# The residual of the first stage enters the down products on TensorE, and GpSimd builds it

## What is computed

```python
# weights are 4-bit codes: _dequant(codes, scales) = table[code] * scale of its block of 64
q, k, v = (_lin_lora(x, W[i], A[i], B[i]) for i in range(3))
attn = (q + k + v) / 3.0
o = _lin_lora(attn, W_o, A_o, B_o)
x1 = x + o
g = _lin_lora(x1, W_g, A_g, B_g)        # 512 -> 1792
u = _lin_lora(x1, W_u, A_u, B_u)
h = silu(g) * u
d = _lin_lora(h, W_d, A_d, B_d)         # 1792 -> 512
x = _layernorm(x + x1 + d)              # stage 1; then a 4-bit linear, an attention, a mixture of experts
```

## Time and profile before

| | |
|---|---|
| Median of 3 runs | 532.95 us (532.86 to 535.76) |
| Profiled execution, span from first to last instruction | 532.1 us |
| PE busy | 494.5 us, 93% |
| DVE busy | 379.4 us, 71% |
| ACT busy | 293.9 us, 55% |
| POOL busy | 251.6 us, 47% |
| Mean granted TensorE clock | 0.993 of full speed |

### The profile page before, as it was taken

One profiled execution on the slowest core, in us unless ns is written; L12 is line 12 of the kernel. 1 busy time (PEld: TensorE's weight loads), 2 busy tenths in 40 slices (PEclk: granted clock), 3 DMA queues, 4 the chain that ended last, 5 costly groups with the idle time before them and its releaser, 6 DMA issues.

```text
span 532.1 us, 7568 instructions
## 1 busy us (share of the span) xinstructions
PE 494.5 (93%) x2278; PEld 394.7 (74%) x2278; DVE 379.4 (71%) x716; ACT 293.9 (55%) x541; POOL 251.6 (47%) x252
## 2 busy tenths in 40 slices
PE   2968999788999999999999999899998899999995
PEld 0236678567888888888888888688886788888874
DVE  4888898666789789797987983577457966366442
ACT  6688856676666576666674742158487422332021
POOL 3357702465566576665674753147479410110001
PEclk9999999899999999999999999999999999999998
DMA  6575421243233333343333300740000000000011
GB/s 169 173 263 159 139 59 41 79 139 100 80 106 75 96 105 118 82 119 97 105 115 97 103 19 0 267 155 5 1 1 1 2 2 19 21 20 22 0 41 39
DMA packets 21415, 43.01 MB, mean 81 GB/s; under 512 B 3328, under 2 KB 3456, under 8 KB 21120
## 3 DMA queue, kind: packets, MB, share of 16 engines
q1 hardware_dynamic: 21152, 42.15, 25.6%
q0 software_dynamic: 224, 0.38, 0.3%
HBM read 40.42 MB, written 2.10 MB: 80 GB/s over the span
## 4 chain that ended last, share of the span: by engine, by line
PE 69%; ACT 3%; issue 3%; DVE 2%; POOL 0%; POOLq 0%; ACTq 0%; DVEq 0%
PE bank L996 62%; PE bank L1162 3%; PE bank L1009 2%; PE bank L1266 1%; ACT prob L957 1%; ACT pT_hi L780 1%; PE bank L1018 0%; DVE rmax L1480 0%; DVE pT_lo L1306 0%; ACT eb_hi L780 0%; ACT bank L785 0%; DVE rows L1413 0%; POOL gu_lo L740 0%; ACT v_hi L780 0%; PE bank L1025 0%
## 5 line engine op out<-in xcount | busy, mean ns | idle before, releaser
L718 POOL TENSOR_TENSOR wf<-value,scale 128x512 f32<-128x512 f32 x50 | 64.5, 1290 | 93.1 <-DVE value L1338 93.1
L996 PE MATMUL bank<-x_hi,gu_hi 128*128 128x512 f32 x224 | 89.9, 401 | 1.7 <-POOL gu_lo L740 1.7
L996 PE MATMUL bank<-x_lo,gu_hi 128*128 128x512 f32 x224 | 88.2, 394 | 0.0
L996 PE MATMUL bank<-x_hi,gu_lo 128*128 128x512 f32 x224 | 88.1, 393 | 0.0
L763 POOL TENSOR_TENSOR rstd<-veps,neg_half 128x1 f32<-128x1 f32 x32 | 17.6, 549 | 121.8 <-issue 110.5
L785 ACT ACTIVATE bank<-code 128x512 f32<-128x512 int32 x124 | 68.7, 587 | 0.0
L1316 DVE SCALAR_TENSOR_TENSOR low<-bent,bank 128x512 f32<-128x512 f32 x62 | 42.5, 685 | 24.0 <-ACT bank L785 19.4
L746 POOL TENSOR_TENSOR h_lo<-act_f,h_hi 128x512 fp32r<-128x512 f32 x28 | 36.3, 1297 | 31.7 <-ACT h_hi L780 31.7
L1413 DVE SCALAR_TENSOR_TENSOR rows<-bank,rows 128x512 f32<-128x512 f32 x48 | 33.0, 688 | 24.7 <-PE bank L996 24.3
L996 PEld LDWEIGHTS bank<-x_hi,gu_hi 128*128 128x128 f32 x224 | 42.6, 190 | 9.9 <-issue 2.1
L996 PEld LDWEIGHTS bank<-x_hi,gu_lo 128*128 128x128 f32 x224 | 42.5, 190 | 9.1
(11 more groups left out here) (198 smaller groups left out, 1172.7 us busy)
## 6 DMA issues: line engine op xcount, KB each, us to landing
code<-codes SPq DMA_DIRECT2D x62, 256.0 KB, 2.7
scale<-scales SPq DMA_DIRECT2D x100, 128.0 KB, 3.0
xs<-xT SPq DMA_DIRECT2D x2, 1024.0 KB, 5.6
ea_raw<-ex_A SPq DMA_DIRECT2D x1, 2048.0 KB, 9.9
eb_raw<-ex_B SPq DMA_DIRECT2D x1, 2048.0 KB, 7.5
out<-rows SPq DMA_DIRECT2D x8, 256.0 KB, 2.0
bgu_raw<-loB_gu SPq DMA_DIRECT2D x1, 896.0 KB, 4.7
wqkv_raw<-w_qkv SPq DMA_DIRECT2D x1, 768.0 KB, 4.3
```

The source lines that it names most:

```text
L718: pool.tensor_tensor(w, v, scale[:, i % RING_CODES, :], ALU.mult).then_inc(scaled_done, 1)
L996: last = nc.tensor.matmul(ps, a, b, start=start and i == 0 and n == 0, stop=stop and i == len(terms) - 1 and n == 2)
```

## The change

Three edits belong together. (1) The item "res" is gone. `down(0, t)` first issues the four transpositions of `xs` for its 128 tokens into its bank, as the start of the accumulation, and the six matmuls add to them. ScalarE then copies the bank to `rows`, where VectorE had added it. (2) The transposed residual can't be divided by GAIN in the bank, so the down weights no longer carry it: their merge divides by GAIN, and the adds of the later rounds lose the factor. (3) VectorE's add of x1 to `xs` is gone. In its place stands an item "xs" in V, at the places that the items "res" had, on which GpSimd adds first `x1_hi` and then `x1_lo` to `xs`; the second add waits for the first. TensorE's waits for `xs_done` ahead of the second batch and of the first products become waits for `x1lo_done` or go; `down(0, t)` waits for `xs_done`. Diff, with unchanged context cut:

```diff
@@ -199,22 +199,22 @@
     half(("u", 1), 0)
     half(("u", 1), 1)
     half(("d", 0), 0)
-    order += [("silu", 0), ("res", 0)]
+    order += [("silu", 0), ("xs", 0)]
     half(("d", 0), 1)
     unit_h(0)
-    order.append(("res", 1))
+    order.append(("xs", 1))
     half(("d", 1), 0)
-    order += [("silu", 1), ("res", 2)]
+    order += [("silu", 1), ("xs", 2)]
     half(("d", 1), 1)
     unit_h(1)
-    order.append(("res", 3))
+    order.append(("xs", 3))
     for f in range(1, NF):
         downs = downs_beside(f) + [None] * 4
         ahead = [(m, f + 1) for m in "gud"] if f < NF - 1 else []
         ahead += [("f", FFN_AT[f])] if f in FFN_AT else []
         halves = [(c, part) for c in ahead for part in range(2)]
         if f == 1:
-            downs = [("res", t) for t in range(TPB, TT)]
+            downs = [("xs", n) for n in range(KT, NB * KT)]
         steps = (("silu", 2 * f), downs[0], ("h", 2 * f), downs[1], ("silu", 2 * f + 1), downs[2],
                  ("h", 2 * f + 1), downs[3])
         if f == 4:
@@ -243,16 +243,11 @@
     return ([None] if f == 2 else []) + downs[max(start, 0):max(start + 4, 0)]
 
 
-def res_beside(f):
-
-    return [("res", 4 * f + i) for i in range(4)] if f < 2 else []
-
-
 def tensor_order():
     order = []
     held = ("d", 1)
     for f in range(NF):
-        downs = (res_beside(f) or downs_beside(f)) + [None] * 4
+        downs = downs_beside(f) + [None] * 4
         ahead = [(m, f + 1) for m in "gud"] if 1 <= f < NF - 1 else []
         late = ("f", FFN_AT[f]) if f in FFN_AT else None
         if f == 0:
@@ -732,6 +726,18 @@
                     pool.wait_ge(xhi_done, item[1] + 1)
                     pool.tensor_tensor(x_lo[:, k, tk], xs[:, k, tk], x_hi[:, k, tk].bitcast(F32), ALU.subtract)\
                         .then_inc(xlo_done, 1)
+                elif kind == "xs":
+                    n = item[1]
+                    b, o = n // KT, n % KT
+                    tk = slice(b * SEQ, (b + 1) * SEQ)
+                    pool.wait_ge(xhi_done, KT * (b + 1))
+                    pool.wait_ge(x1hi_done, n + 1)
+                    pool.tensor_tensor(xs[:, o, tk], xs[:, o, tk], x1_hi[:, o, tk].bitcast(F32), ALU.add)\
+                        .then_inc(xs_step, 1)
+                    pool.wait_ge(x1lo_done, n + 1)
+                    pool.wait_ge(xs_step, n + 1)
+                    pool.tensor_tensor(xs[:, o, tk], xs[:, o, tk], x1_lo[:, o, tk].bitcast(F32), ALU.add)\
+                        .then_inc(xs_done, 1)
                 elif kind == "split":
                     c = item[1]
                     hi, lo = dest(c)
@@ -870,11 +876,11 @@
                     act.wait_ge(x1_ready, NB * KT)
                     copy(la_fhi[:, :], la_f[:, :], fprep_hi)
                     copy(lb_fh[:, :], lb_f[:, :], fprep_hi)
-                elif kind == "res":
-                    t = item[1]
-                    act.wait_ge(res_ready, t + 1)
+                elif kind == "down" and not item[1]:
+                    t = item[2]
+                    act.wait_ge(down_ready, t + 1)
                     act.wait_ge(bprep_done, 2)
-                    copy(rows[:, t, :], bank[7][:, :], res_set)
+                    copy(rows[:, t, :], down_bank(0, t)[:, :], down_added)
                 elif kind == "silu":
                     n = item[1]
                     act.wait_ge(gate_ready, n + 1)
@@ -1085,7 +1091,7 @@
             for n in range(KT, NB * KT):
                 r = n - KT
                 pe.wait_ge(x1hi_done, n - 3)
-                pe.wait_ge(xs_done, n - 3)
+                pe.wait_ge(x1lo_done, n - 3)
                 cut = slice(r * P, (r + 1) * P)
                 product(mm_ps[r][:, :], [(m1_hi[:, k, cut], m1_lo[:, k, cut], x_hi[:, k, SEQ:], x_lo[:, k, SEQ:])
                                          for k in range(KT)]).then_inc(x1_ready, 1)
@@ -1101,7 +1107,6 @@
                     seen = (KT + 1, KT + 2, NB * KT)[m]
                     pe.wait_ge(x1hi_done, seen)
                     pe.wait_ge(x1lo_done, seen)
-                    pe.wait_ge(xs_done, seen)
                 elif m > 2 and g == 0:
                     pe.wait_ge(h_done, n - 1)
                 elif m > 2:
@@ -1116,8 +1121,6 @@
 
                 n = gi * TT + t
                 last_f = GROUPS[gi][-1]
-                if n == 0:
-                    pe.wait_ge(res_set, TT)
                 if gi == len(GROUPS) - 1 and t == 1:
                     pe.wait_ge(h_done, 2 * NF)
                 elif gi == len(GROUPS) - 1 and t > 1:
@@ -1130,29 +1133,20 @@
                 pe.wait_ge(lo_done, split_no(("d", last_f)))
                 tk = slice(t * P, (t + 1) * P)
                 ps = down_bank(gi, t)
+                if gi == 0:
+                    pe.wait_ge(xs_done, KT * (t // TPB + 1))
+                    for k in range(KT):
+                        nc.tensor.matmul(ps[:, k * P:(k + 1) * P], xs[:, k, tk], ident[:, :], is_transpose=True,
+                                         start=k == 0, stop=False)
                 product(ps[:, :], [(h_hi[:, f % RING_H, tk], h_lo[:, f % RING_H, tk],
                                     wd_hi[:, f % RING_H, :], wd_lo[:, f % RING_H, :])
-                                   for f in GROUPS[gi]]).then_inc(down_ready, 1)
-
-            def res(t):
-
-                pe.wait_ge(xs_done, NB * KT)
-                pe.wait_ge(x1hi_done, NB * KT)
-                pe.wait_ge(x1lo_done, NB * KT)
-                if t:
-                    pe.wait_ge(res_set, t)
-                tk = slice(t * P, (t + 1) * P)
-                for k in range(KT):
-                    last = nc.tensor.transpose(bank[7][:, k * P:(k + 1) * P], xs[:, k, tk], ident[:, :])
-                last.then_inc(res_ready, 1)
+                                   for f in GROUPS[gi]], start=gi > 0).then_inc(down_ready, 1)
 
             for item in filter(None, T):
                 if item[0] == "lora":
                     lora(item[1])
                 elif item[0] == "down":
                     down(item[1], item[2])
-                elif item[0] == "res":
-                    res(item[1])
                 else:
                     unit(item[1], item[0] == "up")
 
@@ -1349,7 +1343,10 @@
                     w = wf[:, j % RING_W, :]
                     weight_wait(dve, c)
                     dve.wait_ge(lora_ready, i + 1)
-                    if c[0] != "f":
+                    if c[0] == "d":
+                        nc.vector.scalar_tensor_tensor(w, w, 1.0 / GAIN, lora_ps[:, :], ALU.mult, ALU.add)\
+                            .then_inc(lora_added, 1)
+                    elif c[0] != "f":
                         nc.vector.scalar_tensor_tensor(w, lora_ps[:, :], GAIN, w, ALU.mult, ALU.add)\
                             .then_inc(lora_added, 1)
                     else:
@@ -1374,8 +1371,6 @@
                     dve.wait_ge(x1hi_done, n + 1)
                     dve.wait_ge(xlo_done, KT * (b + 1))
                     rest(x1_lo[:, o, tk], mm_ps[n % 4][:, :], x1_hi[:, o, tk], x1lo_done)
-                    nc.vector.tensor_tensor(xs[:, o, tk], mm_ps[n % 4][:, :], xs[:, o, tk], ALU.add)\
-                        .then_inc(xs_done, 1)
                 elif kind == "bprep":
 
                     i = item[1]
@@ -1402,16 +1397,13 @@
                     dve.wait_ge(unit_ready, n + 1)
                     nc.vector.scalar_tensor_tensor(a, unit_ps[(2 * n + 1) % 3][:, :], 1.0 / GAIN, a, ALU.mult, ALU.mult)\
                         .then_inc(h_done, 1)
-                elif kind == "down":
+                elif kind == "down" and item[1]:
                     gi, t = item[1:]
                     n = gi * TT + t
                     dve.wait_ge(down_ready, n + 1)
-                    if gi == 0:
-                        dve.wait_ge(res_set, t + 1)
-                    else:
-                        dve.wait_ge(down_added, (gi - 1) * TT + t + 1)
-                    nc.vector.scalar_tensor_tensor(rows[:, t, :], down_bank(gi, t)[:, :], 1.0 / GAIN, rows[:, t, :],
-                                                   ALU.mult, ALU.add).then_inc(down_added, 1)
+                    dve.wait_ge(down_added, (gi - 1) * TT + t + 1)
+                    nc.vector.tensor_tensor(rows[:, t, :], down_bank(gi, t)[:, :], rows[:, t, :], ALU.add)\
+                        .then_inc(down_added, 1)
 
             for item in TAIL:
                 kind = item[0]
@@ -1420,8 +1412,7 @@
                     n = gi * TT + t
                     dve.wait_ge(down_ready, n + 1)
                     dve.wait_ge(down_added, (gi - 1) * TT + t + 1)
-                    nc.vector.scalar_tensor_tensor(rows[:, t, :], down_bank(gi, t)[:, :], 1.0 / GAIN, rows[:, t, :],
-                                                   ALU.mult, ALU.add)\
+                    nc.vector.tensor_tensor(rows[:, t, :], down_bank(gi, t)[:, :], rows[:, t, :], ALU.add)\
                         .then_inc(down_added, 1)
                 elif kind == "stat":
```

(3 more changed lines are left out.)

## The result

| | before | changed | ratio, 95% interval |
|---|---|---|---|
| first comparison, median | 533.91 us (4 runs) | 551.73 us (548.83 to 551.85, 4 runs) | 1.0306 [1.0274, 1.0339] |
| second comparison, median | 534.70 us (27 runs) | 548.12 us (546.68 to 549.72, 4 runs) | 1.0246 [1.0209, 1.0282] |
| span of the first profiled execution | 532.1 us | 546.9 us | |

The page of the changed kernel, part 1, answers to the earlier trace rows: TensorE is busy 5.2 us longer in a span that is 14.8 us longer, VectorE has 10.8 us less to do and GpSimd 19.2 us more.

The account below looks back on a forecast made before the run. GpSimd's program order was taken to delay TensorE, which then runs without gaps: 7.96 queue + 2.13 clock + 3.6 transpositions + 1.0 ScalarE = 14.7 us on a 532.1 us span, 546.8, written as time 547.5 us, range 540 to 552.

Parts of the forecast that it names:

- GpSimd's queue: GpSimd from 94.2 us: 16 instructions plus eight add pairs take 41.0 us; f = 2's first up product starts 7.96 us later.
- Clock: TensorE's pauses before f = 2's first up product lower its clock for about 4.26 us behind them: 2.13 us lost.
- Transpositions: Eight groups of four now stand in TensorE's first down round, without gaps, at 0.45 us each: 3.6 us.
- ScalarE's new place: ScalarE's copies wait for TensorE's down groups, delaying later up weights: about 1.0 us of TensorE stall.
- The sum: Whole span: 7.96 + 2.13 + 3.6 + 1.0 = 14.7 us on 532.1, giving 546.8 us.
- From span to time: Whole kernel: the median of the runs stands 0.85 us above the span, so 546.8 becomes 547.6, written 547.5.
- the case that the queue binds: GpSimd's instruction order sets the start of f = 2's first up product as worked out: 542 to 551 us, chance 0.78.
- not slower: Rival: adds hide in GpSimd's idle time; 532 us, or 524 to 528 with all earlier TensorE pauses gone; chance 0.09.
- the GpSimd queue fills less: Rival: GpSimd's adds take 1.04 us each; about 543 us, or 541 without clock loss; chance 0.08.
- Stretched adds: Rival: GpSimd's adds meet VectorE's two-SBUF-input instructions and take 7.4 us more in all, 555 us; chance 0.05.

Follow-up runs that it names:

- the run with one add: Changed kernel with one GpSimd add for each xs item instead of two, the low part of x1 left out: 538.16 us, ratio 1.0076 to before.
- the filler run: Changed kernel with idle matmuls into unused bank 7 in TensorE's three pauses, GpSimd's queue untouched: 549.05 us, ratio 1.0293 to before.
- the items apart: Changed kernel with the xs items moved in the order, none beside the LoRA factor preparation on VectorE, two late: 539.38 us, ratio 1.0078 to before.
- the run with the items spread: Changed kernel with the same sixteen adds moved to places where GpSimd had been idle: 537.28 us, ratio 1.0055 to before.
- the run with dprep later: Changed kernel, x1 added by VectorE, fprep earlier, plus LoRA down-factor preparation moved behind the merge of g 1: 535.42 us, ratio 1.0017 to before.

## Why the prediction was right, and where it was off

The forecast was slower, 547.5 us, between 540 and 552; measured were 551.73 and 548.12. By its steps, in the first profile:

- **GpSimd's queue.** Predicted 41.0 us from 94.2, up 4 at 135.35, 7.96 us late; measured 41.23 us from 94.21, up 4 at 135.59, 8.20 us late. The pair took 2.68 us against 2.62: the adds are 1.285 us as the row of the same operation said, but between the two there are 0.15 us (98.19 - 96.76 - 1.28) where the nearest row had 0.08. Against VectorE's 0.682 us the ratio is 1.9, so the row gave the sum. The Trainium skill, GPSIMD Engine Reference, section 4.1 (Engine selection), calls GpSimd about 2x slower for two inputs; the trace agrees nearly, with 1.9. That the queue and not the rest of the change sets up 4 was argued then; the run with x1 on VectorE and the run with one add show it.
- **Clock.** Predicted 2.13 us, measured 4.44 - 2.85 = 1.6. The sign and the mechanism hold (the filler run); the size was misread. I took half of the 4.26 us, as if all of it ran at the lower level, but the mean clock of that row is 0.62, which loses 0.38 x 4.26 = 1.6 us. The pauses were not where I had put them: about 5.5, 3 and 4 us, and in the trace 5.55 before the lora step ahead of up 3, 0.83 before gate 4, and 5.79 before up 4. I had not reckoned that up 3 itself runs slow and fills the gap before gate 4. That the row of 1.9 us without loss gives no bound for pauses under 3 us is shown by the runs with one add (2.98 us) and with the items apart (2.24 us), which both lost clock, and a longer pause gives no certainty either (the last section).
- **Transpositions.** Predicted 3.6 us. From up 4 to up 8 the trace has 41.45 us against 35.06 before: 6.39 more, of which 1.6 are clock and 0.82 the wait of up 8, so 3.97. Leaving them out gave back 2.74, with 3.37 less busy time of TensorE and 0.63 more idle time. The estimate lies between 3.37 and 3.97; they are on the path nearly one for one.
- **ScalarE's new place.** Predicted 1.0 us at up 8, measured 0.82; that fprep behind the seventh copy is the cause is shown by moving it.
- **The sum** was 14.7 us, and the spans differ by 546.9 - 532.1 = 14.8. That it fits so closely is in part luck: the 0.5 us too much for the clock and 0.2 too much for up 8 stand against 0.2 too little for the queue and 0.4 for the transpositions, and the two executions happened to begin alike (74.41 and 74.42 us), where others began up to 2.1 us later.
- **From span to time** is the term that was mis-sized. I added 0.85 us, the distance from the one span to the median of three runs that were not it. Where a span and its own run's time are both known they lie 1.9 to 2.0 us apart (548.83 and 546.9; 532.78 and 530.8). So the profiled execution of before stood for about 534.1 us, and 546.8 for 548.8: the profiled run took 548.83. The rest, up to 551.85, is spread between executions, which I had not put into the sum at all. The upper end of 552, which no term of the sum had set, is only 0.3 us above the first median. The base moved too: the kernel before had medians of 533.91 and 534.70 us beside these runs, not 532.95, so the forecast difference of 14.6 us stands against 17.8 and 13.4.

Two figures of the prediction do not follow from its own working: the low end of the case that the queue binds is 543.7, not 542, and the terms named for *not slower* with all pauses gone give 523, not 524 to 528. Neither touches the result.

Of the rivals, *the GpSimd queue fills less* asked for adds of 1.04 us; they took 1.285. *Not slower* asked for adds of about 0.53 us each; half the adds, which is 0.63 each for sixteen, still gave 1.0076. *Stretched adds* did not happen where the change put them, but they do exist: the run with the items spread met them.

## What to carry to other kernels

An engine that is half idle on average can still be full where the work is put: before work is moved to it, count its queue from the instruction that starts the stretch to the one that the bottleneck waits for, in program order, and compare with how long that stretch lasts now. Work that was free in a stretch with pauses costs nearly its full price in a stretch without them: with x1 added by VectorE, up 4 came 4.5 us sooner than before the change, and 4.8 us were lost behind it. When an order is written by hand, a better slot read from the old trace moves as soon as the stretch gets shorter; look for who needs the result first, and for who shares a resource with it in that slot.

## What the runs showed of the hardware that I had not expected

VectorE and GpSimd hold each other up when VectorE reads both operands from SBUF: the two dprep instructions went from 1.15 and 1.28 us to 2.30 and 2.31 beside GpSimd's adds, and two of the adds from 1.29 to 1.95 and 2.25. Not every add pays: the one at 91.27 us, beside the first dprep instruction, took 1.29. VectorE's instructions with one operand in PSUM stayed at 0.68 to 0.69 us through the whole stretch in which GpSimd was never idle, so the changed kernel itself did not pay this. One of them, beside GpSimd's add at 102.14 us in the first profile of the changed kernel:

```profile
102.88 0.69 DVE L1332 SCALAR_TENSOR_TENSOR value<-bank,low 128x512 f32<-128x512 f32 x1
```

The Trainium skill, Advanced Engine Details and Errata, section GPSIMD Details, says that GpSimd shares a read and a write interface with VectorE and conflicts with its instructions that have two SBUF inputs; these rows agree and give the size.

The length of a pause of TensorE does not tell by itself whether it costs clock, and the fall can come after the work has resumed. Behind 2.98 us the clock was 1.00 at the restart and 0.61 in the mean of the next 4.41 us; behind 2.24 us it fell about 1 us after the restart; a pause of 1.75 us cost nothing. But the same wait of 2.16 us at the lora step of u 1 was followed by the lower level in the changed kernel and by the full clock with x1 on VectorE, and a wait of 3.29 us, in the run with dprep later, cost nothing. Also with x1 on VectorE, the clock fell about 1.2 us behind the restart after a wait of only 1.57 us. Stretches of TensorE behind these four waits (us, busy by engine, granted clock), in this order:

```profile
94.78:98.00 3.22, 3.22 (x10) 2.74 (x11) 2.22 (x4) 3.16 (x6) 3.18 (x3) 0.50 0.27 64
...
93.73:97.92 4.19, 3.46 (x17) 2.62 (x17) 3.18 (x6) 3.17 (x6) 2.58 (x3) 1.00 0.34 73
...
100.06:104.50 4.44, 4.43 (x19) 3.68 (x20) 2.96 (x5) 3.69 (x7) 3.27 (x3) 1.00 0.24 59
...
108.42:113.00 4.58, 4.58 (x15) 3.73 (x16) 3.59 (x6) 3.20 (x6) 3.62 (x4) 0.63 0.47 125
```

What decides it, no run here shows. In the two waits of over 5 us in the first profile of the changed kernel, 5.55 and 5.79, the clock fell within the wait.
